# Transposes of the softmax weights in a cross-attention and mixture-of-experts kernel: two row tiles of 64 tokens into two PSUM banks, in place of one of 128

## The reference

```
x = x + tanh(g_xattn) * xattn(layernorm(x), ctx)
x = x + tanh(g_ffn)   * ffn(layernorm(x))

xattn: q = LN(x) Wq, k = LN(ctx) Wk, v = LN(ctx) Wv      # 16 heads of 64, 64 context rows
       softmax(q k^T / 8) v, heads joined, times Wo
ffn:   shared = (sum over 2 shared experts of gelu(x sw1 + sb1) sw2 + sb2) / 2
       gates = x router_w + router_b, the best 2 of 8 experts, softmax over the two
       sum over the chosen of prob * (gelu(x w1 + b1) w2 + b2)
```

## Time and profile before

| | us |
|---|---|
| median of 3 runs | 380.45 (380.31 to 381.46) |
| span of the profiled execution | 378.1 |
| TensorE matmuls busy | 370.8 (98%) |
| TensorE loads busy | 352.3 (93%) |
| VectorE busy | 282.0 (75%) |
| ScalarE busy | 241.7 (64%) |
| GpSimd busy | 221.4 (59%) |

### The profile page before, as it was taken

The page is one execution under the profiler, slowest core; times in us unless marked ns, Lnnn a source line. Parts: engine busy times, 40 slices in busy tenths (PEclk is TensorE's granted clock), DMA queues, the critical chain, the costliest instruction groups (busy, mean ns, idle before and its releaser), DMA issues.

```text
span 378.1 us, 8799 instructions
## 1 busy us (share of the span) xinstructions
PE 370.8 (98%) x2773; PEld 352.3 (93%) x2774; DVE 282.0 (75%) x612; ACT 241.7 (64%) x540; POOL 221.4 (59%) x262
## 2 busy tenths in 40 slices
PE   8999999999999999999999999999999999999996
PEld 7898989999999989999999999999999997999995
DVE  5798799978988988799898897555556555554486
ACT  3666545665665545787878757766666665777850
POOL 8367657688878764377885226546565655653200
PEclk9999999999999999999999999999999999999999
DMA  7990000001000048511940022222223233650397
GB/s 219 313 340 6 2 14 29 16 21 35 14 14 14 29 142 333 222 32 14 300 138 2 14 46 84 80 63 85 83 79 89 85 84 111 210 144 30 110 350 251
DMA packets 33839, 40.15 MB, mean 106 GB/s; under 512 B 9674, under 2 KB 26508, under 8 KB 33676
## 3 DMA queue, kind: packets, MB, share of 16 engines
q1 hardware_dynamic: 28960, 29.40, 25.0%
q0 software_dynamic: 4768, 10.28, 8.9%
q10 hardware_dynamic: 76, 0.02, 0.0%
HBM read 27.88 MB, written 11.68 MB: 105 GB/s over the span
## 4 chain that ended last, share of the span: by engine, by line
PE 91%; DVE 2%; POOL 2%; issue 2%; DMA 1%; ACT 1%; DVEq 0%; POOLq 0%
PE psum L1336 12%; PE psum L1359 12%; PE psum L1296 10%; PE psum L1252 10%; PE psum L1504 8%; PE psum L1598 8%; PE psum L1478 6%; PE psum L1559 6%; PE psum L1219 3%; PE psum L1138 2%; PE psum L1176 2%; PE psum L1200 2%; PE psum L1583 2%; PE psum L1284 1%; PE psum L1491 1%
## 5 line engine op out<-in xcount | busy, mean ns | idle before, releaser
L743 POOL DMA_INDIRECT y_tok<-ysl,table x39 | 38.9, 996 | 41.7 <-ACT ysl L1029 36.5
L736 POOL DMA_INDIRECT xsl<-y_rows,table x39 | 38.7, 991 | 30.0 <-PE psum L1359 9.6
L709 POOL DMA_INDIRECT names<-named,pos x32 | 37.5, 1170 | 12.8 <-issue 7.9
L662 POOL TENSOR_TENSOR Eb<-Eb,rinv 128x512 f32<-128x512 f32 x32 | 33.5, 1065 | 13.1 <-DVE rinv L1810 13.1
L1073 ACT ACTIVATE hr<-psum,b_cur 128x256 f32<-128x256 f32 x48 | 20.1, 470 | 22.1 <-DVE b_cur L2103 12.3
L905 ACT ACTIVATE yTb<-psum 128x256 f32<-128x256 f32 x16 | 6.2, 385 | 42.7 <-PE psum L1316 42.7
L1598 PE MATMUL psum<-xsT_hi,w_cur 128*128 128x256 f32 x192 | 31.0, 284 | 0.0
L645 POOL TENSOR_TENSOR half_sum<-Eb 128x512 f32<-128x512 f32 x16 | 20.6, 1287 | 12.0 <-ACT Eb L860 11.8
L1598 PEld LDWEIGHTS psum<-xsT_hi,w_cur 128*128 128x128 f32 x192 | 26.5, 192 | 0.0
L2152 DVE TENSOR_TENSOR hr_lo<-hr,hr_hi 128x512 fp32r<-128x512 f32 x24 | 16.6, 692 | 13.2 <-ACT hr_hi L1086 13.0
L940 ACT ACTIVATE early_stage<-psum,vec_col 128x256 f32<-128x256 f32 x48 | 20.0, 467 | 8.8 <-PE psum L1336 8.0
(11 more groups left out here) (276 smaller groups left out, 1255.9 us busy)
## 6 DMA issues: line engine op xcount, KB each, us to landing
w_raw<-in_L_ffn_w SPq DMA_DIRECT2D x2, 4096.0 KB, 15.6
y_got<-y_tok SPq DMA_DIRECT2D x8, 512.0 KB, 8.3
xs_all<-in_x SPq DMA_DIRECT2D x4, 512.0 KB, 12.3
sw_raw<-in_L_ffn_sw SPq DMA_DIRECT2D x2, 1024.0 KB, 13.8
y_rows<-ybuf SPq DMA_DIRECT2D x16, 128.0 KB, 1.7
sw_lo_kept<-sw_lo SPq DMA_DIRECT2D x1, 2048.0 KB, 6.6
sw_lo<-sw_lo_kept SPq DMA_DIRECT2D x8, 256.0 KB, 3.1
out<-xs_all SPq DMA_DIRECT2D x3, 512.0 KB, 3.1
```

What stands on the lines that cost most here:

```text
L662: nc.gpsimd.tensor_tensor(Eb[q][:, heads, :], Eb[q][:, heads, :], rinv[:, q, heads].unsqueeze(2).broadcast_to([P, H // 2, CTX]), ALU.mult) ...
L709: nc.gpsimd.indirect_dma_start(names, bass.IndirectOffsetOnAxis(ap=pos[:, k, t:t + 1], axis=0), named[:, k, t, :], None).then_inc(scattere ...
L736: nc.gpsimd.indirect_dma_start(into[:, s % 2, :], None, y_rows, bass.IndirectOffsetOnAxis(ap=table[:, s, 0:1].bitcast(I32), axis=0)).then_ ...
L743: nc.gpsimd.indirect_dma_start(y_tok, bass.IndirectOffsetOnAxis(ap=table[:, s, 1:2].bitcast(I32), axis=0), ysl[:, s % 2, :], None).then_in ...
```

## The change

Each piece of two heads is transposed in two halves: tokens 0 to 63 (partitions 0 to 63) against the upper left quarter of the identity into bank 6, and tokens 64 to 127 against the lower right quarter into bank 7. A half has 64 rows, 128 stationary columns and 64 moving ones. So there are sixteen transposes a tile in place of eight, and a bank now holds all heads of 64 tokens, in place of half the heads of 128 tokens. Both banks are full only after the last piece, and `pt_psum` is raised by the last two transposes. Since bank 7 is written from piece 0 on, the wait for `yt_ready` stands ahead of piece 0. Ahead of pieces 0 and 4 TensorE's queue raises a semaphore `half_begun`, for which nobody waits; the wait for `p_ready` is placed ahead of it. ACT's copies and DVE's subtraction go over the same elements with other strides. The values are the same.

```diff
+        half_begun = sem("half_begun")
...
-                    for g in range(2):
-                        act.wait_ge(pt_psum, i * 2 + (g + 1))
-                        last = nc.scalar.activation(pt_hi[:, g * 4:(g + 1) * 4, :],
-                                                    bank[6 + g][:, :].rearrange("p (c n) -> p c n", c=4), ACT.Copy)
+                    for r in range(2):
+                        act.wait_ge(pt_psum, i * 2 + (r + 1))
+                        last = nc.scalar.activation(pt_hi[:, :, r * P // 2:(r + 1) * P // 2],
+                                                    bank[6 + r][:, :].rearrange("p (c n) -> p c n", c=NPAIR), ACT.Copy)
                     last.then_inc(pt_hi_ready, 1)
...
                         for c in range(NPAIR):
                             if c == 0 and fixed == 0:
                                 pe.wait_ge(vw_lo, VW_BANKS.index(7) + 1)
+                            if c == 0 and (fixed is None or i >= 2):
+                                pe.wait_ge(yt_ready, i - 1)
                             if c % 4 == 0:
                                 pe.wait_ge(p_ready, i * 2 + (c // 4 + 1))
-                            if c == NPAIR // 2 and (fixed is None or i >= 2):
-                                pe.wait_ge(yt_ready, i - 1)
-                            last = nc.tensor.transpose(bank[6 + c // 4][:, (c % 4) * P:(c % 4 + 1) * P],
-                                                       Eb[par][:, 2 * c:2 * c + 2, :].rearrange("p h j -> p (h j)"), ident[:, :])
-                            if c % 4 == 3:
-                                last.then_inc(pt_psum, 1)
+                                pe.sem_inc(half_begun, 1)
+                            for r in range(2):
+                                rows = slice(r * P // 2, (r + 1) * P // 2)
+                                last = nc.tensor.transpose(bank[6 + r][:, c * P // 2:(c + 1) * P // 2],
+                                                           Eb[par][rows, 2 * c:2 * c + 2, :].rearrange("p h j -> p (h j)"),
+                                                           ident[rows, rows])
+                                if c == NPAIR - 1:
+                                    last.then_inc(pt_psum, 1)
...
-                    nc.vector.tensor_tensor(pt_lo[:, :, :], psum[:, 6 * BANK:8 * BANK].rearrange("p (c n) -> p c n", c=NPAIR),
-                                            pt_hi[:, :, :].bitcast(F32), ALU.subtract).then_inc(pt_lo_ready, 1)
+                    nc.vector.tensor_tensor(pt_lo[:, :, :].rearrange("p c (r n) -> p c r n", r=2),
+                                            psum[:, 6 * BANK:8 * BANK].rearrange("p (r c n) -> p c r n", r=2, c=NPAIR),
+                                            pt_hi[:, :, :].bitcast(F32).rearrange("p c (r n) -> p c r n", r=2), ALU.subtract
+                                            ).then_inc(pt_lo_ready, 1)
```

## The result

The change takes 382.13 us (median of 7 runs, 381.44 to 383.24) against 380.45 (380.31 to 381.46): a ratio of 1.0039, 95% interval 1.0022 to 1.0057. In a second set of runs it was 382.19 (12 runs) against 380.89, ratio 1.0024, 1.0004 to 1.0044. (The ratios are estimated from all the runs of both kernels, so they are not exactly the ratios of the medians.) So it is slower by 0.2 to 0.4%; the two intervals reach from 0.04 to 0.57%. The predicted 381.9 us lies within 0.3 us of both, but only part of its working holds.

The account below looks back on a forecast made before the run. TensorE, busy 98% of the span, was taken to bound the kernel. +1.0 us over fourteen steps, +0.2 late normalisations and +0.2 ramp gave +1.4: span 379.5, time 381.9 us, own range 379.9 to 384 (8 in 10: 379.4 to 387.4).

Parts of the forecast that it names:

- The body: Each attention step's transposes on TensorE: sixteen halves for eight, both tiles loading and streaming side by side, 0.38 us less.
- Rival A: Transposes in each step: the two tiles' loads don't overlap; step +0.41 us, time 386.9 us; chance 0.35.
- 107 ns a load: Transposes in each step, by the skill's page: body 0.86 us, step +0.28, time about 384.8 us; not taken.
- The switches: TensorE going from 128 rows to 64 and back once per step: 0.15 us each way, +0.30 together.
- The feed: TensorE's queue handing out 32 instructions within each step's transposes at 0.02 us each: +0.15 us a step.
- B: Transposes in each step: tiles side by side, queue doesn't limit; -0.09 us a step, time 379.2 us; chance 0.15.
- the wait at c = 0: TensorE's `yt_ready` wait ahead of each step's transposes: hidden by 0.04 us under the change to 64 rows.
- The circle: Later ACT copies delaying POOL's normalisation: 0.3 us later against 0.4 in hand; +0.2 us in all for two late steps.
- The ramp: Attention's start (49 to 57 us), where TensorE waits for normalised weights: 0 to 0.4 us extra, taken as +0.2.
- Behind the attention: After 150 us TensorE has hardly a gap until the last stores, so earlier changes pass to the end nearly whole.

Follow-up runs that it names:

- 40 skipped: Changed kernel with 40 never-executed instructions that TensorE jumps over behind the loop: 380.58 us, ratio 1.0006 to the kernel before (run again on a chip with usual times).
- late_copies: Kernel before, with ACT waiting for both banks ahead of its first copy to `pt_hi` too: 384.14 us, ratio 1.0076.
- wait_first: Kernel before, whole transposes, with TensorE's wait for `yt_ready` moved to c = 0 and `half_begun` added: 382.77 us, ratio 1.0042.
- 216 skipped: Kernel before with 216 never-executed instructions that TensorE jumps over behind the loop: 381.41 us against 380.57, ratio 1.0016 (run again on a chip with usual times).
- short_copies: Changed kernel with ACT copying only the first four column groups of each bank to `pt_hi` from step 2 on: 382.39 us, ratio 1.0041.

## Why the prediction came out right, step by step

**The body, -0.38 a step: right.** Two tiles load side by side, a pair every 0.061 us. Rival A, given a chance of 0.35, fell. The sentence of the Trainium skill (TensorEngine Tiling (Array Packing), Key Properties) that different tiles load and multiply in parallel agrees with these loads. The 107 ns a load that I had worked out, as an estimate, from the rule of the Trainium skill (TensorE: Matmul & The Clock Gate, LDWEIGHTS) does not, since eight pairs take 0.49 us and not 0.86.

**The switches, +0.30: right,** within 0.01 us: in the changed kernel (0.15 out) and doubled (0.41 with the transpose). In the loop the switch in can't be read by itself, since the moved wait lies beside it. The price came from a single 44-row transpose in the prologue.

**The feed, +0.15: wrong.** The queue hands out 32 instructions and the increment in at most 0.43 us (88.27 to 88.70, with the tiles' pace in it), so 0.013 each or less, where I took 0.02. The reading of 0.04 from two waits was too high; perhaps it held time in which the queue had nothing to hurry for, which was not tested. The rival without this limit (B, 0.15) therefore describes the body better, except that the wait at c = 0 sticks out by 0.04 us and the first pair starts ragged: 1.08 for 1.09 us by the chain, not 0.09 less. In the step at 58 us the wait isn't in the way (the first load starts 0.21 us behind the last product in place of 0.24 to 0.28), and from the last product to L1238's first it is 0.91 us in both profiles, 0.07 less than in the loop: there B's 0.09 is gained. In the written-out steps at 125 and 140 us the block is 0.04 to 0.07 us shorter than in the kernel before.

**The circle, +0.2: undersized, and it ran past the place that I looked at.** I had followed the later copies to POOL's normalisation and found 0.4 us in hand. But behind the normalisation POOL has `xn_lo` (L672), and DVE has the subtraction that frees the scores' banks (L1839), and TensorE's scores wait for both. POOL's `xn_lo` ends at 88.30 + 0.73 = 89.03 and DVE's subtraction at 87.84 + 1.23 = 89.07, and the scores start at 89.16; in the kernel before, in the step of the earlier trace rows, they ended at 88.23 and 88.28, and the scores started at 88.64.

```profile
87.84 1.23 DVE L1839 TENSOR_TENSOR Eb<-psum,mx 128x1024 f32<-128x1024 f32 x1
...
88.30 0.73 POOL L672 TENSOR_TENSOR xn_lo<-xn_raw,xn_hi 128x256 fp32r<-128x256 f32 x1
...
89.16 0.71 PE L1257 MATMUL psum<-A_hi,xn_hi 128*128 128x512 f32 x2
```

The cover was 0.36 us and the delay is 0.24 to 0.27. In most steps that is hidden. In the step that opens a turn of the loop the queue has register work of its own behind these waits (a row of L1257 in TensorE's queue from 96.57 to 96.68, behind POOL's and DVE's ends at 96.44 and 96.48), and there it costs 0.17 to 0.19 us. The larger part is lost elsewhere: in step 12, the first behind the loop, TensorE's transposes of `ybuf` (L1321) wait, and that costs 0.3 us in both profiles of the kernel after, in the one with 40 skipped too, and nothing in the kernel with the short copies. DVE has been 0.3 us late since its sum of the step before, which waits for POOL's half sum behind ACT's later copies and exponentials, and from there to `ybuf` it has no idle time to make that up. In the kernel before, `ybuf` was ready at 130.65 and the transposes started at 130.79, with no wait; in the kernel after:

```profile
131.32 0.35 DVE L1753 TENSOR_SCALAR ybuf<-xs_all,mv,r 128x256 f32<-128x256 f32 x1
...
131.82 0.30 PE L1321 MATMUL psum<-ident,ybuf 128*128 128x128 f32 x1 [0.15 <-DVE ybuf L1753]
```

These two places make 0.48 us; the other seven steps change by under 0.07 us each. Over nine steps the loss is 0.44 to 0.54 us, and over the fourteen that I summed about 0.7 to 0.8. My +1.0 for the feed and +0.2 for two late normalisations were meant for other causes; together they overstate it by more than half.

**The ramp, +0.2: wrong in sign, -0.4.** The exponentials come later there, and POOL's half sum with them. It no longer runs beside DVE's `zbuf`, which takes 0.40 us in place of 1.50; in the kernel before, then after:

```profile
52.58 1.50 DVE L1777 TENSOR_SCALAR zbuf<-xs_all,mv,r 128x256 f32<-128x256 f32 x1
...
52.64 1.29 POOL L645 TENSOR_TENSOR half_sum<-Eb 128x512 f32<-128x512 f32 x1 [1.68 <-ACT Eb L860]
```

```profile
53.57 0.40 DVE L1782 TENSOR_SCALAR zbuf<-xs_all,mv,r 128x256 f32<-128x256 f32 x1
...
54.04 1.29 POOL L646 TENSOR_TENSOR half_sum<-Eb 128x512 f32<-128x512 f32 x1 [2.09 <-ACT Eb L861]
```

No kernel was made to test it, but the profiles of the others agree: `zbuf` takes 0.40 us and TensorE gains 0.3 to 0.7 us from 51 to 59 us wherever the half sum starts 0.4 us or more behind it (also in `late_copies` and `wait_first`, which have no half transposes), and it takes 1.5 us, with nothing gained, wherever the half sum starts within 0.1 us (the kernel before, again and with 216 skipped, and `short_copies`).

**Behind the attention, nothing forecast: +1.5 to 2.0 in the profiles.** I had taken the time after 160 us as passed on unchanged. With the placing of the code undone, the change is worth what the steps above make: -0.4 up to the fourth step, +0.5 over the nine steps, nothing behind them, 0.16 us in all by the profile, and 1.0006 (0.9992 to 1.0021) by the clock. Between 148 and 160 us both profiles of the kernel after lose 0.6 us, and both profiles with 40 instructions skipped lose 0.2. Most of the difference is one wait for ACT's `early_hT_hi` at 161 us, where 0.3 us is lost. The code's placing alone doesn't explain it: the kernel before with 216 skipped loses nothing there, and `late_copies`, with the kernel before's code on TensorE, loses 0.3. Its cause stays open.

So the sum of +1.4 was met by +1.7, and that close only by luck. The body and the switches nearly cancel, as forecast; but the feed doesn't limit, the ramp gives where it was to cost, the circle costs more than its +0.2, and in the profiles nearly all of the difference arises where nothing was forecast (0.1 to 0.2 us at 148 us, 2.3 and 2.6 at 345). Errors of 0.4 to 2 us in both directions made up for each other.

## What to carry to other kernels

Two row tiles of 64 rows do load and multiply side by side, but a block of them must be long enough to pay two switches of 0.15 us: here 0.38 is gained against 0.30 and a few hundredths for the wait and the first pair, which leaves next to nothing. When a copy moves later, follow it not to the first engine that has time in hand but once round to the instruction it started from, and take the smallest cover on the way. When a change alters the number of instructions and the loss turns up far behind it, skip a matching number of them before believing in either kernel: by the profiles a fetch of code beside transfers that others wait for cost 1.5 to 2.0 us here, as much as the whole measured difference.

## What the hardware showed that I had not expected

- Loads of two row tiles that stand one tile after the other in the program still overlap in part (0.88 us for sixteen, against 0.61 alternating and 1.06 in a row, the last a sum and not a run).
- From the end of the instruction that a wait is for (ACT's copy) to the first load behind it: 0.22 us, with `half_begun` behind it in the queue.
- A DVE operation of 0.40 us (`zbuf`) took 1.50 us when a POOL operation of 1.29 us (the half sum) started 0.06 us behind it.
- A scatter issued at 318.2 us took 5.8 us to land with a fetch of code at 321.1, and 4.2 us where the fetch came 1.7 us ahead of it. Fifteen of its sixteen landing signals were there after 4.3 us.
- The prologue's transfers alone move the first scores by up to 4 us from run to run.
